# A hybrid of two attentions and feed-forwards on one core: more buffers between the stages, other instructions for two small steps, new lists of work

## What is computed

```python
x = x + attn_a(layernorm(x))     # per batch, N = 256, D = 128
x = x + ffn(layernorm(x))        # hidden 384, integer weights / 127
x = x + attn_b(layernorm(x))     # 16 heads of 64, causal softmax
x = x + ffn(layernorm(x))

def attn_a(x):
    Q, K, V = (sigmoid(4 * (batchnorm(x @ W) - 1)) for W in (Wq, Wk, Wv))
    tq, tk = 1 - mean(Q), 1 - mean(K)            # one number per row
    d = tq[:, None] - tk[None, :]
    f = 0.9 * exp(-2 * abs(d))
    return (where(d < 0, f, -f) + 0.9) @ V @ Wo + bo

def ffn(x):
    return (silu(x @ wg.T) * (x @ wu.T)) @ wd.T

def attn_b(x):                                   # per head
    p = softmax(causal(q @ k.T / 8))
    return sum_over_heads(p @ v @ Wo) + bo
```

## Time and profile before

| | |
|---|---|
| runs, median (lowest to highest) | 334.21 us (333.73 to 335.56) |
| profiled execution | 333.27 us |
| its span, first to last instruction | 331.2 us |
| TensorE matmuls (PE), busy | 313.8 us, 3256 instructions |
| VectorE (DVE), busy | 267.9 us, 1092 |
| ScalarE (ACT), busy | 230.8 us, 784 |
| GpSimd (POOL), busy | 201.2 us, 265 |
| DMA | 5.83 MB, nearly all in the first 17 us |

### The profile page before, as it was taken

One profiled execution on the slowest core, in us unless ns is written; L12 is line 12 of the kernel. 1 busy time (PEld: TensorE's weight loads), 2 busy tenths in 40 slices (PEclk: granted clock), 3 DMA queues, 4 the chain that ended last, 5 costly groups with the idle time before them and its releaser, 6 DMA issues.

```text
span 331.2 us, 9981 instructions
## 1 busy us (share of the span) xinstructions
PE 313.8 (95%) x3256; PEld 274.8 (83%) x3256; DVE 267.9 (81%) x1092; ACT 230.8 (70%) x784; POOL 201.2 (61%) x265
## 2 busy tenths in 40 slices
PE   1897999999999999999999999999999999999996
PEld 1686888889888998788898897889888998888785
DVE  4677899968988879879889897968988697977545
ACT  2663679777968768686878677667768849687721
POOL 4468676776655757675698487553565484437700
PEclk9999999999999999999999999999999999999999
DMA  6900000000000000000000000000000000000001
GB/s 195 306 0 3 3 1 3 2 1 3 2 2 4 0 2 18 0 3 3 0 19 4 2 0 4 2 16 2 4 18 0 3 3 18 3 0 3 3 0 49
DMA packets 6418, 5.83 MB, mean 18 GB/s; under 512 B 864, under 2 KB 5856, under 8 KB 6368
## 3 DMA queue, kind: packets, MB, share of 16 engines
q1 hardware_dynamic: 6080, 4.99, 5.0%
q10 hardware_dynamic: 288, 0.20, 0.2%
HBM read 4.15 MB, written 1.05 MB: 16 GB/s over the span
## 4 chain that ended last, share of the span: by engine, by line
PE 76%; DVE 8%; issue 6%; POOL 5%; ACT 3%; DMA 1%; DVEq 0%; ACTq 0%; POOLq 0%
PE bank L512 11%; PE bank L477 7%; PE bank L440 7%; PE bank L341 7%; PE bank L489 7%; PE bank L342 6%; PE bank L343 6%; PE bank L411 5%; PE bank L474 5%; PE bank L401 3%; PE bank L402 3%; PE bank L359 2%; PE bank L390 2%; POOL wqkv_lo L849 1%; DMA x<-x_in 1%
## 5 line engine op out<-in xcount | busy, mean ns | idle before, releaser
L862 POOL TENSOR_TENSOR prob<-prob,row_inv 128x256 f32<-128x256 f32 (+1 forms) x128 | 103.7, 836 | 62.4 <-DVE row_inv L775 62.3
L603 ACT ACTIVATE prob<-neg_s,neg_max 128x256 f32<-128x256 f32 x128 | 63.8, 499 | 0.0
L601 ACT ACTIVATE prob<-neg_s,neg_max 128x128 f32<-128x128 f32 x128 | 50.5, 395 | 12.3 <-DVE neg_max L760 11.8
L760 DVE CUSTOM_DVE_ANT_0 neg_s<-bank,mask 128x256 f32<-128x256 f32 x128 | 53.6, 419 | 0.0
L611 ACT ACTIVATE prob_t<-bank 128x384 f32<-128x384 f32 x64 | 29.5, 484 | 26.3 <-PE bank L489 26.3
L512 PE MATMUL bank<-prob_t,v 128*64 128x256 f32 (+1 forms) x512 | 47.1, 331 | 0.1
L758 DVE CUSTOM_DVE_ANT_0 neg_s<-bank,mask 128x128 f32<-128x128 f32 x128 | 36.5, 285 | 12.5 <-PE bank L477 10.5
L785 DVE TENSOR_TENSOR qk<-bank,bqk 128x512 f32<-128x512 f32 x64 | 42.4, 683 | 3.8 <-PE bank L343 3.7
L512 PEld LDWEIGHTS bank<-prob_t,v 128*64 128x64 f32 x512 | 32.1, 136 | 13.6 <-issue 3.2
L768 DVE COPY prob_t<-bank 128x384 f32<-128x384 f32 x64 | 34.0, 551 | 6.4 <-PE bank L489 6.2
L477 PE MATMUL bank<-qk 64*128 64x256 f32 x256 | 38.7, 377 | 0.0
(11 more groups left out here) (146 smaller groups left out, 781.4 us busy)
## 6 DMA issues: line engine op xcount, KB each, us to landing
wqkv<-wqkv_in SPq DMA_DIRECT2D x3, 512.0 KB, 6.9
x<-x_in SPq DMA_DIRECT2D x8, 128.0 KB, 5.7
out<-x SPq DMA_DIRECT2D x8, 128.0 KB, 1.8
wo<-wo_in SPq DMA_DIRECT2D x1, 512.0 KB, 6.9
wa<-wa_in ACTq DMA_DIRECT2D x1, 192.0 KB, 3.2
wg_i<-wg_in SPq DMA_DIRECT2D x1, 192.0 KB, 3.4
wu_i<-wu_in SPq DMA_DIRECT2D x1, 192.0 KB, 3.3
wd_i<-wd_in SPq DMA_DIRECT2D x1, 192.0 KB, 3.7
```

Source lines behind the costliest of these rows:

```text
L601: nc.scalar.activation(prob[:, r, e, 0:P], neg_s[:, m % 2, e, 0:P], ACT.Exp, bias=neg_max[:, q, 2 * e:2 * e + 1], scale=-1.0, accum_out=ro ...
L603: nc.scalar.activation(prob[:, r, e, P:SC], neg_s[:, m % 2, e, P:SC], ACT.Exp, bias=neg_max[:, q, 2 * e + 1:2 * e + 2], scale=-1.0, accum_ ...
L760: nc.vector.tensor_tensor_reduce(out=neg_s[:, m % 2, e, P:SC], in0=S[:, P:SC], in1=mask[:], scale=-SCORE_SCALE, scalar=3e38, op0=ALU.add, ...
L862: nc.gpsimd.tensor_tensor(pr, pr, inv, ALU.mult).then_inc(p_norm, 1)
```

## The change

- Rings: qk 3 to 4 buffers, neg_s 2 to 3, prob and its small companions 4 to 6, prob_t 4 to 8. Four of the eight prob_t buffers lie over wqkv (now a view of `early`); the first job that writes there, number 4, waits for all six low parts (`weights_split`).
- Epsilon: mv is a view of one tile with a third column that holds epsilon, written once by a memset; variance plus epsilon is a tensor_reduce over the last two columns.
- Comparison: VectorE compares the mean straight from the PSUM bank by two tensor_scalar instructions and releases the bank after them. A semaphore of its own (`mean_s`) tells ScalarE that tq and tk are there. tk keeps its sign and the distance is taken with scale -1.
- Jobs: normalising on VectorE (`xnA.0`, `xnF.0`, `xnB.0`, `xnP.7`), the preparation of attention A's constants (`ga`, `gb`), the casts of the feed-forward weights (`wf`) and xb on GpSimd (`xb`) are jobs of their own. The subtractions w0, w2 and w4 are on VectorE, w1, w3 and w5 stay on GpSimd. There are 14 hot jobs instead of 12.
- All lists in `ORDER` and all banks in `BANKS` are new.

The diff, with the lists cut to their starts and the pieces that the text speaks of:

```diff
+QK_BUFS, SCORE_BUFS, PROB_BUFS, PT_BUFS = 4, 3, 6, 8
...
     "PE": """
-        lntA.0 hot.0 qkv1.0 qkv0.0 qkv2.0 mean.0 lntA.1 vwo.0 hot.1 hot.2 hot.3 qkv1.1 aout.0 qkv0.1 qkv2.1 hot.4 hot.5 mean.1
-        lntF.0 hot.6 hot.7 gF1.0 gF0.0 gF2.0 bo.0 lntA.2 dbF.0 qkv1.2 qkv0.2 vwo.1 qkv2.2 aout.1 lntB.0 hot.8 qk.0 qk.1 v1.0
-        scores.0 scores.1 lntF.1 qk.2 qk.3 qk.4 gF2.1 v3.0 gF0.1 gF1.1 qk.5 scores.2 scores.3 transposes.0 dbF.1 v0.0 mean.2
+        hot.0 hot.1 hot.2 hot.3 hot.4 lntA.0 hot.5 qkv0.0 qkv1.0 qkv2.0 mean.0 lntA.1 vwo.0 hot.6 hot.7 qkv2.1 aout.0 qkv0.1
+        vwo.1 qkv1.1 hot.8 mean.1 lntF.0 hot.9 hot.10 gF2.0 gF0.0 gF1.0 bo.0 lntA.2 dbF.0 aout.1 qkv1.2 qkv2.2 hot.11 lntB.0
+        qkv0.2 hot.12 qk.0 qk.1 qk.2 lntF.1 scores.0 scores.1 gF2.1 gF1.1 gF0.1 v3.0 qk.3 qk.4 qk.5 scores.2 scores.3 scores.4
...
     "DVE": """
-        lnsA.0 lntA.0 lnsA.1 mean.0 sign.0 lntA.1 lnsA.2 aout.0 lnsF.0 bv.0 lntF.0 mean.1 gF1.0 gF0.0 gF2.0 sign.1 bo.0 lntA.2
-        dbF.0 lnsB.0 aout.1 lntB.0 lnsF.1 qk.0 qk.1 mask.0 mask.1 lntF.1 qk.2 qk.3 qk.4 inverse.0 gF2.1 gF0.1 gF1.1 mask.2
+        lnsA.0 ga.0 xnA.0 lnsA.1 lntA.0 gb.0 mean.0 w0.0 sign.0 lntA.1 wf.0 aout.0 lnsF.0 lnsA.2 xnF.0 bv.0 lntF.0 mean.1 gF2.0
+        gF0.0 gF1.0 w2.0 sign.1 lntA.2 dbF.0 lnsB.0 aout.1 bo.0 xnB.0 lnsF.1 lntB.0 w4.0 qk.0 qk.1 qk.2 lntF.1 mask.0 mask.1
...
     "POOL": """
-        lnsA.0 lnsA.1 sv.0 stdp.0 lnsF.0 lnsA.2 w5.0 sv.1 w0.0 stdp.1 w2.0 lnsB.0 w1.0 w4.0 lnsF.1 sv.2 w3.0 norm.0 norm.1 bo.0
+        lnsA.0 ga.0 lnsA.1 sv.0 stdp.0 xb.0 sv.1 xb.1 lnsF.0 lnsA.2 w1.0 stdp.1 xb.2 lnsB.0 lnsF.1 sv.2 w5.0 w3.0 norm.0 norm.1
...
+        early = sb("early", [P, 3 * H * A])
+        wqkv = early[:].rearrange("p (w n) -> p w n", w=3)
...
+        mv_eps = sb("mv_eps", [P, 4, T, 3])
+        mv = {k: mv_eps[:, i, :, :] for i, k in enumerate("AFBP")}
...
+        prob_t = sb("prob_t", [P, PT_BUFS // 2, 2, SC])
+        prob_t_late = early[:].rearrange("p (m e s) -> p m e s", m=PT_BUFS // 2, e=2)
...
+        def weights_split(eng, m):
+
+            if m == PT_BUFS // 2:
+                for i in range(6):
+                    eng.wait_ge(w_lo[i], 1)
...
-                        last = nc.scalar.activation(dist[:, j, :], tq[:, b % 2, :], ACT.Abs, bias=ntk[:, b % 2, j:j + 1])
+                        last = nc.scalar.activation(dist[:, j, :], tq[:, b % 2, :], ACT.Abs, bias=tk[:, b % 2, j:j + 1], scale=-1.0)
...
+            link(nc.vector.memset(mv_eps[:, :, :, 2:3], EPS))
...
-                    nc.vector.scalar_tensor_tensor(var[c][:], mv[c][:, :, 1], EPS, mv[c][:, :, 1], ALU.add, ALU.max).then_inc(var_s[k], 1)
...
+                    nc.vector.tensor_reduce(out=var[c][:], in_=mv[c][:, :, 1:3], axis=mybir.AxisListType.X, op=ALU.add).then_inc(var_s[k], 1)
...
-                    nc.vector.tensor_scalar(ntk[:, b % 2, :], src[:, N:N + T], 0.5, -1.0, ALU.add, ALU.mult).then_inc(free, 1)
-                    freed(dve, job, b)
+                    nc.vector.tensor_scalar(tk[:, b % 2, :], src[:, N:N + T], 0.5, None, ALU.add).then_inc(mean_s, 1)
+                    dve.wait_ge(mean_s, b + 1)
...
-                        last = nc.vector.scalar_tensor_tensor(less[:, j, :].rearrange("p (k s) -> p k s", s=P), tq[:, b % 2, :].rearrange("p (k s) -> p k s", s=P),
-                                                              ntk[:, b % 2, j:j + 1], mask[:, 0:P].unsqueeze(1).to_broadcast([P, T, P]), ALU.add, ALU.is_lt)
-                    last.then_inc(less_s, 1)
...
+                        last = nc.vector.tensor_scalar(less[:, j, :], src[:, 0:N], 0.5, tk[:, b % 2, j:j + 1], ALU.add, ALU.is_lt)
+                    last.then_inc(free, 1)
...
-                    if m >= 2:
-                        dve.wait_ge(p_exp[e], m - 1)
...
+                    if m >= SCORE_BUFS:
+                        dve.wait_ge(p_exp[e], m - SCORE_BUFS + 1)
```

More of the change, by code:

```diff
@@ L54 @@
[L54 to L66, removed]
@@ L109 @@
-        inverse.1 mask.3 qk.5 dbF.1 inverse.2 lnsB.1 pt1.0 pt1.1 mask.4 mask.5 pt1.2 inverse.3 mean.2 qk.6 inverse.4 qk.7
-        inverse.5 lntB.1 pt1.3 mask.6 pt1.4 mask.7 sign.2 qk.8 qk.9 inverse.6 qk.10 aout.2 lnsF.2 mask.8 pt1.5 pt1.6 inverse.7
-        mask.9 qk.11 qk.12 lnsA.3 inverse.8 pt1.7 lntF.2 mask.10 mask.11 inverse.9 gF2.2 pt1.8 qk.13 gF1.2 gF0.2 inverse.10
-        inverse.11 lntA.3 qk.14 dbF.2 lnsB.2 mask.12 mask.13 out0.0 pt1.9 out1.0 inverse.12 pt1.10 lnsP.0 pt1.11 qk.15 mean.3
@@ L117 @@
-        qk.26 pt1.20 pt1.21 aout.4 inverse.23 lnsF.4 gP0.1 gP2.1 mask.24 mask.25 qk.27 inverse.24 pt1.22 pt1.23 lntF.4 mask.26
-        mask.27 pt1.24 lnsA.6 inverse.25 lntA.5 gF0.4 out0.2 gF1.4 pt1.25 gF2.4 inverse.26 qk.28 qk.29 gP1.1 dbF.4 inverse.27
-        lnsB.4 mask.28 mask.29 mean.5 qk.30 qk.31 pt1.26 pt1.27 out1.2 lnsP.2 mask.30 lntB.4 lntA.6 mask.31 inverse.28
-        inverse.29 inverse.30 sign.5 qk.32 qk.33 dbP.1 inverse.31 lntP.2 mask.32 mask.33 pt1.28 aout.5 pt1.29 lnsF.5 qk.34 gP2.2
@@ new lines @@
+        aout.2 pt1.4 lnsF.2 lnsA.3 pt1.5 inverse.7 inverse.8 qk.10 qk.11 qk.12 lntF.2 pt1.6 pt1.7 mask.10 pt1.8 lnsA.4 mask.11
+        gF2.2 gF1.2 gF0.2 out0.0 inverse.9 lntA.3 qk.13 inverse.10 dbF.2 lnsB.2 mask.12 mask.13 inverse.11 qk.14 inverse.12
+        pt1.9 lntB.2 out1.0 mean.3 inverse.13 qk.15 qk.16 pt1.10 pt1.11 mask.14 mask.15 sign.3 pt1.12 inverse.14 lnsP.0 pt1.13
+        aout.3 qk.17 inverse.15 lnsF.3 lntP.0 mask.16 mask.17 pt1.14 pt1.15 qk.18 gP2.0 inverse.16 lntF.3 qk.19 qk.20 gP1.0
@@ new lines @@
+        gP0.0 gF2.3 inverse.17 lntA.4 gF0.3 pt1.16 mask.18 mask.19 pt1.17 lnsA.5 gF1.3 qk.21 out1.1 inverse.18 inverse.19 out0.1
+        lnsP.1 dbF.3 lnsB.3 lnsA.6 mask.20 mask.21 pt1.18 pt1.19 qk.22 mean.4 dbP.0 inverse.20 qk.23 lntB.3 sign.4 mask.22
+        mask.23 inverse.21 qk.24 qk.25 lntP.1 aout.4 lnsF.4 pt1.20 pt1.21 mask.24 inverse.22 mask.25 inverse.23 inverse.24
+        lntF.4 qk.26 lntA.5 qk.27 qk.28 gP2.1 gP0.1 inverse.25 pt1.22 pt1.23 mask.26 mask.27 pt1.24 pt1.25 qk.29 inverse.26
@@ new lines @@
+        inverse.27 qk.30 gF1.4 gF2.4 gF0.4 gP1.1 pt1.26 dbF.4 mask.28 pt1.27 out0.2 lnsB.4 mask.29 mean.5 qk.31 out1.2 lntB.4
+        mask.30 inverse.28 mask.31 inverse.29 qk.32 qk.33 sign.5 lntA.6 lnsP.2 mask.32 inverse.30 lnsA.7 mask.33 pt1.28
+        inverse.31 aout.5 qk.34 lnsF.5 pt1.29 pt1.30 dbP.1 pt1.31 qk.35 lntP.2 inverse.32 qk.36 inverse.33 lntF.5 gP0.2 gF1.5
+        gP2.2 gF0.5 gF2.5 pt1.32 pt1.33 mask.34 mask.35 mask.36 dbF.5 lnsB.5 qk.37 qk.38 mask.37 inverse.34 lntB.5 mean.6 gP1.2
@@ L584, in side @@
                 elif job == "dist":
-                    freed(act, "mean", b)
+                    act.wait_ge(mean_s, b + 1)
                     if b:
```

344 lines of the change are left out of this document (181 added, 163 removed).

## The result

Four runs of the changed kernel take 326.60 to 327.21 us, median 326.65; four of the kernel before, beside them, 333.73 to 335.56, median 334.45. The ratio is 0.977, interval 0.975 to 0.980. The forecast was 329.4 with a range of 326.0 to 333.6: the sign is right, and of the 7.8 us that went it had 4.8. The profiled execution lasts 326.63 us with a span of 324.4, so 6.8 less than the span before; it stands for the median. The kernel before was profiled in one of its shorter executions (333.27 against the median of 334.45), so the traces show 6.8 us of the 7.8; run 1 shows where the rest may lie.

What follows compares the result with a forecast made beforehand. It took TensorE (PE) as the bound, asking where it is not fed. From 333.27 us it subtracted 2.0 (head), 0.8 (width changes) and 2.0 (stalls), giving 328.5; with 0.94 up to the median, 329.4, range 326.0 to 333.6.

Steps and rivals of the forecast that it cites:

- At most 2.7 us leave the path: Head: fewer POOL subtractions ahead of lnsB.0 and a shorter var_B start rstd_B earlier; 0.87 us taken.
- The warm TensorE: Head: hot jobs ahead of lntA.0 save 0.22 us on two transposes and about 0.3 on a qkv job's matmuls.
- first transposes pair at 0.44: Head, sign of being right: the first two transposes take 0.44 us together instead of 0.66.
- DVE gains 5 us; outside the head they lie beside a busy PE: Epsilon steps by tensor_reduce at 0.16 us each: DVE gains 5 us, outside the head beside a busy PE.
- DVE gains 3.6 us, hidden: Comparison from PSUM, 16 at 0.42 us instead of 0.648: DVE gains 3.6 us, hidden.
- The 2.8 us that I gave to PE's order: Body: 0.8 us from fewer changes between full and 64-wide work, 2.0 us from stalls before transposes.
- Worth little directly; worth what they allow PE's order to do: Rings: full buffers hardly show as waits (DVE 1.0 us for neg_s); extra buffers matter through PE's order.
- Stalls: 40 to 320 us: 24 late PE jobs, 7.1 us, nine before transposes with 2.6; 2.0 us go, bounds -1.5 and +5.5.
- rival 4: Slower: DVE releases the mean bank late, PE stands 0.84 us in 8 batches, stalls stay; 338.1 us, chance 0.08.
- rival 3: Head given back: two DVE subtractions meet two-tensor POOL instructions, 2.0 us eaten, no stall goes; 333.4 us, chance 0.08.
- rival 1: Banks limit, not buffers: head and width changes come, stalls only move; 331.4 us, chance 0.20.
- rival 2: Deep pipeline: all 7.1 us of late jobs go and the head gives 3.0; 323.3 us, chance 0.06.

Runs made afterwards that it cites:

- run 1: The kernel before with the larger rings alone (qk 4, neg_s 3, prob 6, prob_t 8), all lists as before: 333.42 us, ratio 0.998.
- run 8: The changed kernel with weight subtractions w0, w2 and w4 back on GpSimd: 326.39 us against 326.65.
- run 11: The changed kernel without the five hot jobs ahead of lntA.0: 329.24 us, 2.6 over the changed kernel.
- run 3: The changed kernel with both old instructions back (epsilon step and comparison): 331.18 us, 4.5 over the changed kernel.
- runs 1 and 2: The second of these: the kernel before with the larger rings, new epsilon step and new comparison, all lists as before: 331.84 us, ratio 0.992.
- run 4: The changed kernel with smaller rings (qk 3, prob 5, prob_t 4; neg_s 3 kept): 331.41 us, 4.8 over the changed kernel.
- run 7: The changed kernel with both old instructions and small rings, leaving new lists, banks and jobs: 335.99 us, ratio 1.005 to the kernel before.
- run 6: The changed kernel with the old comparison alone, from SBUF with the mean bank released early: 329.56 us, 2.9 over the changed kernel.
- run 9: The changed kernel with prob_t at 4 buffers, none over the dead weights: 329.61 us, 3.0 over the changed kernel.

## Why the prediction was right or wrong

**Sign and forecast.** Right: faster. The time is 2.8 us below the forecast, near the lower end of the range, and two terms carry that: the body was to give 2.8 us and gave 4.7, and the profile's 0.94 up to the median was no longer there (326.63 against 326.65). The sums of the prediction come out as written. That the total lies in the range is in part luck: in the head two wrong terms make a right sum, and in the body a term taken at nothing was worth 4.5 us.

**Head.** The sum is right (2.0 forecast, 1.88 came), its composition is wrong. "At most 2.7 us leave the path", of which I took 0.87 for the epsilon step and the subtractions on POOL: with the subtractions back qk.0 moves by 0.17, and with both old instructions by 0.08. POOL is free in time for rstd_B either way, since its stdp.1 comes at 25.51 (25.10 in run 8) instead of 27.37 on the new lists. The warm TensorE, which I gave 0.22 and 0.3 us, is worth 2.7 (run 11). I had scaled it by the pair of transposes and three matmuls of the one trace, in which PE reached its full rate at 10.3 us; without hot jobs ahead it can stay slow to 17 us and more. In the profiled run 1 on the old lists it did (qk.0 at 33.61). Run 1 and run 11, which have a late turn to full rate in common (16.55 and 18.68 us) and differ in lists and instructions, are 0.6 us apart at qk.0. So more of the head's gain is the warming than the lists, some 1.3 of the 1.9 us if those 0.6 are theirs, which is argued from single traces; and how much it is differs with the execution. The sign "first transposes pair at 0.44" was wrong for the profiled execution (0.66).

**Instructions.** "DVE gains 5 us; outside the head they lie beside a busy PE" and "DVE gains 3.6 us, hidden" are the steps that failed. The sizes were near: 0.157 where I took 0.16, 0.48 where I took 0.42, and a DVE total 5.1 us lower, where I had named less than some 6 as a sign of being wrong; the comparison gives 2.7 and not 3.6, and two casts are 0.8 longer together. But hidden they are not: on these lists they are worth 1.9 and 2.9 us, 4.5 together. The 2.8 us that I gave to PE's order come only with them: with both old instructions the body is 285.5, against 285.7 before the change (run 3). I asked whether PE was busy beside them, and not who is queued behind the few long ones; the time of DVE is hidden on average, and not at the dozen places where rt_lo, a mask or a norm is due. In the old lists the same edits are worth about 1.6 (runs 1 and 2).

**Rings.** "Worth little directly; worth what they allow PE's order to do": both halves hold, 1 us at most with the old lists (run 1), 4.8 with the new (run 4), against rings that were still partly enlarged. What I did not see is that the lists are a loss without them: the part of the change that I gave most of the gain is by itself 1.5 us slower than before (run 7). Lists alone +1.5, the rest alone -2.6, together -7.8: the gain sits in the combination, some 6.7 us of it. By the bodies alone, which leave the head's variation out, it is +4.8, -1.7 and -4.7.

**Stalls.** I let 2.0 us go. By the same count of PE's jobs as in the prediction, 20 jobs are late by over 0.15 us instead of 24, 4.3 us together instead of 7.1, so 2.8 went; those in front of transposes fell from 9 with 2.6 us to 4 with 1.0. The largest left in the body are 0.45 us, where there had been 0.83. The count hangs on which neighbours are called alike: with jobs told apart by their own kind and the next one's alone, the same two traces give some 12 and 9 us, with both neighbours' kinds 3.8 and 3.2. So 7.1, 4.3 and their difference are rough. The order of neighbours would then have the rest of the body, 4.7 - 2.8 = 1.9, against my 0.8; that is argued, no run parts it from the lists.

**Rivals.** The slower mean bank (rival 4) does not show: no wait of PE for a bank behind mean, and run 6, which releases it early again, loses. The head was not given back (rival 3): DVE's three subtractions took 0.68 each, the duration that I had taken, and met nothing. Banks as the limit (rival 1) would have left 331.4 us with the stalls only moved; 326.65 came, and in run 9 a ring in SBUF alone moves 3 us. The deep pipeline (rival 2) was the nearest of the four to the time that came, 3.3 us below the median, but neither did all late jobs go nor did the head give 3.0.

**What stays open.** Which of the new places in the lists, and how much the new banks, make the combination worth more than its parts, and whether another order would need the rings less. How the time of the kernel before divides over its kinds of heads. The tail's 0.3 us was not looked into.

## To carry to other kernels

Where engines work through fixed lists, price a slower instruction or a full ring by what stands behind it in the same list, for a dozen places, and not by whether the bottleneck is busy beside it: two comparisons 1.2 us longer on an engine that is 81% busy came out as 0.86 us in which TensorE stood. An order, its buffers and the speed of the small steps are one thing: test the order with the buffers of before as well, since each may be nothing or a loss alone. And give TensorE matmuls that nobody reads while it has nothing to do: without the five such jobs ahead, five executions took 1.0 to 2.7 us longer than the median with them.
